# Edge products ahead of pair 0's main product in the opening of four convolution phases

## What is computed

```python
def _layer(x, style, w, b, mw, mb, typ):
    s = style @ mw.T + mb
    weight = SCALE * w * s[:, None, :, None]
    demod = lax.rsqrt(jnp.sum(weight * weight, axis=(2, 3)) + EPS)
    weight = weight * demod[:, :, None, None]
    ...   # 'same' conv; 'upsample': transposed conv and blur; 'downsample': blur and strided conv
x = x + L0_ffn(L0_cond(x, cond_512, ...))   # fp8 quantised product, 1024 x 1024
x = x + L1_ffn(L1_cond(x, cond_512, ...))   # base product and 16 experts of rank 64, top 2
x = x + L2_ffn(L2_cond(x, cond_512, ...))   # base product, 8 experts of rank 16, sparsemax gate
x = x + L3_ffn(L3_cond(x, cond_512, ...))   # low-rank gated (silu) ffn, 1024-256-5504-256-1024
```

## Time and profile before

| | us |
|---|---|
| three executions: median (lowest to highest) | 2113.85 (2109.53 to 2119.47) |
| the profiled execution, its own time | 2111.62 |
| its span, from first to last instruction | 2109.6 |
| TensorE busy | 1958.6 (93% of the span) |
| VectorE, ScalarE, GpSimd busy | 1302.2, 960.7, 374.2 |
| mean granted TensorE clock | 0.971 of full speed |

### The profile page before, as it was taken

The page is one execution under the profiler, slowest core; times in us unless marked ns, Lnnn a source line. Parts: engine busy times, 40 slices in busy tenths (PEclk is TensorE's granted clock), DMA queues, the critical chain, the costliest instruction groups (busy, mean ns, idle before and its releaser), DMA issues. The chain is left out here.

```text
span 2109.6 us, 31997 instructions
## 1 busy us (share of the span) xinstructions
PE 1958.6 (93%) x10128; PEld 1661.1 (79%) x10128; DVE 1302.2 (62%) x2326; ACT 960.7 (46%) x1547; POOL 374.2 (18%) x457
## 2 busy tenths in 40 slices
PE   4899968799999979998899999988999999999999
PEld 4677733699999877887688888877888778878886
DVE  6888888867776753336766666656555433343343
ACT  4477754455545431113444444424666544433442
POOL 4122211211111100002111111112121222222221
PEclk9899989899999989998899999998999999999999
DMA  7566646322112254434211121223333211142114
GB/s 195 179 183 184 177 155 227 108 74 76 60 60 78 62 174 141 144 118 147 94 60 60 60 70 61 64 63 118 100 100 108 89 47 45 52 141 85 50 45 163
DMA packets 118608, 222.30 MB, mean 105 GB/s; under 512 B 18336, under 2 KB 65184, under 8 KB 117792
## 3 DMA queue, kind: packets, MB, share of 16 engines
q1 hardware_dynamic: 102048, 212.36, 32.1%
q10 hardware_dynamic: 16512, 9.31, 1.6%
HBM read 159.04 MB, written 62.59 MB: 105 GB/s over the span
## 5 line engine op out<-in xcount | busy, mean ns | idle before, releaser
L125 POOL TENSOR_TENSOR rows<-l_EY,ones 128x4 f32<-128x4 f32 x128 | 36.0, 281 | 780.9 <-ACT rows L1331 420.4
L2647 DVE SCALAR_TENSOR_TENSOR f_prod<-ps,b,f_gate 128x512 f32<-128x512 f32 (+1 forms) x88 | 66.0, 750 | 171.6 <-ACT f_gate L2587 171.6
L2688 POOL TENSOR_TENSOR x_lo<-f_prod,x_hi 128x512 fp32r<-128x512 f32 (+1 forms) x88 | 104.9, 1192 | 290.5 <-ACT x_hi L2594 290.5
L2517 PE MATMUL ps<-pt_hi,v_hi 128*128 128x512 f32 (+1 forms) x352 | 138.7, 394 | 2.3 <-PEq L631 1.7
L2517 PE MATMUL ps<-pt_lo,v_hi 128*128 128x512 f32 (+1 forms) x352 | 138.3, 393 | 0.0
L2517 PE MATMUL ps<-pt_hi,v_lo 128*128 128x512 f32 (+1 forms) x352 | 137.7, 391 | 0.0
L1079 PE MATMUL ps<-l_u_hi,l_g_hi 128*128 128x512 f32 x272 | 115.2, 424 | 20.2 <-DVE l_u_lo L1535 10.2
L2587 ACT ACTIVATE f_gate<-ps,b 128x512 f32<-128x512 f32 (+1 forms) x88 | 60.5, 688 | 158.8 <-PE ps L2517 158.8
L1559 DVE SCALAR_TENSOR_TENSOR rows<-ps,dem3e,l_middle 128x512 f32<-128x512 f32 x60 | 45.1, 751 | 119.5 <-ACT l_middle L1300 97.2
L125 POOL TENSOR_TENSOR XE<-rows,ones 128x8 f32 (+1 forms) x96 | 21.0, 242 | 531.3 <-DVE rows L1769 256.1
L1079 PE MATMUL ps<-l_u_lo,l_g_hi 128*128 128x512 f32 x272 | 111.1, 408 | 0.0
(11 more groups left out here) (402 smaller groups left out, 5819.7 us busy)
## 6 DMA issues: line engine op xcount, KB each, us to landing
x<-rows SPq DMA_DIRECT2D x64, 512.0 KB, 2.9
xin<-x SPq DMA_DIRECT2D x96, 256.0 KB, 4.1
rows<-x SPq DMA_DIRECT2D x48, 512.0 KB, 4.0
out<-rows SPq DMA_DIRECT2D x32, 512.0 KB, 2.6
v<-in_ffn_v SPq DMA_DIRECT2D x84, 128.0 KB, 2.6
xin<-in_x SPq DMA_DIRECT2D x16, 512.0 KB, 5.4
xb<-in_x SPq DMA_DIRECT2D x16, 512.0 KB, 3.3
x<-xb SPq DMA_DIRECT2D x16, 512.0 KB, 2.6
```

The lines of the kernel that those rows point to most:

```text
L125: return g.tensor_tensor(dst, src, one.broadcast_to(src.shape), ALU.mult)
L2517: mm = nc.tensor.matmul(ps[0:m, 2 * g + gu, :], v1sp[ws][:, s, r, gu, 0:m], pt[ms][:, r, cols], start=(k == 0), stop=(k == 5))
L2647: v.scalar_tensor_tensor(prod[0:m, g, :], ps[0:m, 2 * g + 1, :], b1[0:m, 1, bass.ds(2 * i + g, 1)], gate[0:m, g, :], ALU.add, ALU.mult).th ...
L2688: nc.gpsimd.tensor_tensor(asp[1][0:m, g, :], prod[0:m, g, :], asp[0][0:m, g, :].bitcast(F32), ALU.subtract).then_inc(al_ready, 1)
```

## The change

- TensorE's `edges_p` writes to banks 7 and 4 in place of 5 and 6 (VectorE reads it there), and waits for both halves of pair 0's `l_u_lo` (`ul_ready`) in place of `g_summed`.
- TensorE's order in the opening becomes `conv0_half(1, 0)`, `edges_p`, `conv0_half(1, 1)`, `edges_v`, `main_half(0, 0)`, `weights_a(2)`, `edges_y`, `main_half(0, 1)`, `weights_g(1)`.
- VectorE does `edges_p` ahead of `split_g(0)`, and `edges_y` ahead of `read_u(1, ...)`.
- GpSimd's first piece of weights waits for `gl_ready` of pair 0.
- ScalarE splits the first weight piece after `cross_g(0)` and not before it; in layers 1 to 3 the pieces that were split between `cross_g(1)` and `split_h(0)` come after it, on ScalarE and VectorE.

```diff
@@ TensorE, edges_p
                 pe.wait_ge(ue_ready, n)
-                pe.wait_ge(g_summed, g0 + 1)
+                pe.wait_ge(ul_ready, 2 * g0 + 2)
...
-                                ps[:, 5 + h, 0:NP * 3 * PW].rearrange("p (n k) -> p n k", k=PW),
+                                ps[:, 7 - 3 * h, 0:NP * 3 * PW].rearrange("p (n k) -> p n k", k=PW),
@@ TensorE, iteration, first
                     conv0_half(1, 0)
                     edges_p()
-                    main(0)
+                    conv0_half(1, 1)
                     edges_v()
-                    conv0_half(1, 1)
+                    main_half(0, 0)
                     weights_a(2)
                     edges_y()
+                    main_half(0, 1)
                     weights_g(1)
@@ ScalarE
             split_x(1)
-            some_chunks(1)
             cross_g(0)
-            some_chunks(1)
+            some_chunks(2)
             split_g(0)
@@ ScalarE, first_pair
                 cross_g(1)
-                if layer > 0:
-                    some_chunks(2 if fast else 1)
-                else:
+                if layer == 0:
                     split_g(1)
                 split_h(0)
-                if layer > 0:
-                    some_chunks(1)
-                    if not fast:
-                        split_g(1)
+                if layer > 0 and not fast:
+                    split_g(1)
                 some_chunks(len(chunks))
@@ VectorE, edges_p
-                        src = ps[rows, 5 + h, 0:NP * 3 * PW].rearrange("p (n s k) -> p n s k", s=3, k=PW)
+                        src = ps[rows, 7 - 3 * h, 0:NP * 3 * PW].rearrange("p (n s k) -> p n s k", s=3, k=PW)
@@ VectorE
             split_x_half(1, 1)
-            split_g(0)
             some_maxima(1)
@@ VectorE, first_pair
                 edges_p()
+                split_g(0)
                 read_a(1)
...
                 edges_v()
+                edges_y()
                 if not fast:
                     read_u(1, 0)
                     read_u(1, 1)
-                edges_y()
...
-                some_chunks(2 if fast else 1)
                 split_h(0)
@@ GpSimd
+            if len(chunks) > 0:
+                pool.wait_ge(gl_ready, g0 + 1)
             for k in range(min(POOL_CHUNKS, len(chunks))):
                 chunk(k)
```

## The result

The changed kernel takes 2123.88 us (median of 19 runs, 2119.80 to 2131.89); the kernel before, run beside it 19 times, 2115.39. The medians differ by 8.5 us; the ratio of the runs is 1.0044, 95% interval 1.0032 to 1.0055, which is 9.3 us. The forecast was 2123.6, +9.7 us over the median of 2113.85 known then. The profiled execution took 2123.05 us with a span of 2121.0, against 2111.62 and 2109.6 before: +11.4.

What follows compares the result with a forecast made beforehand. VectorE, never idle in the opening, was taken to bound the kernel. Layer terms 4.0 + 0 + 3.0 + 2.7 gave +9.7 us over the 2113.85 median, 2123.6 us; forecast's own range 2119 to 2128, whole range 2112 to 2132.

Steps and rivals of the forecast that it cites:

- Up to `ve_ready`: VectorE's chain from layer start to `ve_ready`: shifts of 0, -0.5, +2.4 and +0.15 us in layers 0 to 3.
- The signs named: Profile signs: no wait ahead of `edges_p`, stretched `split_z` and first piece, two TensorE waits of 2 to 6 us per opening.
- The turns of the two engines: GpSimd and VectorE alternate instruction by instruction outside PSUM; each GpSimd weight piece takes 2.37 us.
- Rival 2: GpSimd's pieces cost VectorE nothing, `ve_ready` comes earlier; -6.3 us, 2107.6 us; chance 0.12.
- The second half on the path: Half product between `edges_y` and `weights_g(1)`: +2.84 us at full clock; 0.78 us of low-clock loss moves, adding nothing there.
- rival 1: Second halves and `weights_g(1)` run cold, losing up to 2.8 us each; +17.7 us in all, 2131.6 us; chance 0.18.
- Layer by layer: Delay of pair 1's start per opening: +4.0, 0, +3.0 and +2.7 us in layers 0 to 3.
- the pieces that leave `split_h(0)`: Layer 1: two weight pieces leave VectorE's way to `split_h(0)`, -2.35 us.
- The stall: Layer 2: pair 1's `l_g_lo`, 3.59 us beside GpSimd's residual sum in place of 1.40, escapes it; -2.2 us.
- The loops: Pair loops: TensorE has no DMA wait, so what pair 1 loses at its start is carried to the end in full.
- rival 3: Loops of layers 0 and 2 absorb the delay; half the sum, +4.8 us, 2118.7 us; chance 0.15.

Runs made afterwards that it cites:

- a1: The changed kernel without GpSimd's wait for `gl_ready`, so its weight pieces start as early as in the kernel before; 1.0005 of the kernel before.
- a3: The changed kernel with no weight piece on GpSimd; VectorE splits all, two ahead of `edges_v`, four behind `edges_y`; 0.9995 of the kernel before.
- a7: The changed kernel with 20 added matmuls ahead of `edges_y` in layers 1 and 2, in the wait for `l_h_lo`; 1.0039 of the kernel before.
- a6: The changed kernel with the later weight pieces back ahead of `split_h(0)` on ScalarE and VectorE in the fast layers; 1.0049 of the kernel before.
- b1: The kernel before with one part of the change, GpSimd's pieces waiting for `gl_ready`; 1.0008 of the kernel before.
- b2: The kernel before with no weight piece on GpSimd, VectorE splitting all of them; 0.9980 of the kernel before.
- c1: All pieces on VectorE; layers 0 and 3 with the kernel before's order, banks and first wait, layers 1 and 2 with the change's; 0.9959 of the kernel before.
- c2: As c1, but layers 1 and 2 have the whole product ahead of `edges_y` and 20 added matmuls ahead of `edges_v`; 0.9964 of the kernel before.
- a8: As a4, with 20 added matmuls into bank 3 ahead of `edges_v` in every layer; 0.9945 of the kernel before.
- a4: The changed kernel with no piece on GpSimd and pair 0's whole product between `edges_v` and `edges_y`; 0.9980 of the kernel before.

## Why the prediction was right, and where it was not

**Up to `ve_ready`: right.** Forecast 0, -0.5, +2.4 and +0.15 us; measured -0.37, -1.20, +1.82 and -0.23. All four are 0.4 to 0.7 us early. In layers 1 and 3, 0.5 and 0.4 of that lie between the ends of `l_g_lo` and `l_h_lo`, where I had added the pieces' time and VectorE's own in full. The signs named came: next to no wait ahead of `edges_p`, `split_z` and the first piece stretched, waits of 4.8 to 5.7 us at line 989 and 1.4 to 5.6 at line 1003 (the forecast said 2 to 6; layers 0 and 3 lie under that). The turns of the two engines, read off one stretched `x_lo`, are borne out by `a1` and, with 4.06, 4.75 and 1.43 us against 4.0, 4.5 and 1.1, by `a3`. Rival 2 (the pieces cost VectorE nothing) is out.

**The second half on the path: right in kind, too small in size.** The step was "+2.84 us at full clock", with the 0.78 us of `weights_g(1)`'s low clock that "moves and adds nothing". From `ve_ready` to the first transpose it took 3.88, 3.82 and 4.17 us more in layers 1 to 3. The halves behind the longer waits lost 1.5 to 1.8 us each, of which `weights_g(1)` gave back 1.0 and 1.3 in layers 1 and 2, where it had been cold before, and nothing in layer 3, where it had been warm. In these three layers that is the mechanism of rival 1 at a half to two thirds of the 2 us per layer it was given; `a7` shows it by taking it away. So the term was sized 1.0 to 1.3 us too small in each of them.

My argument for the small size was that a wait of 1.33 us had not brought the lower level. It rested on layer 3 alone. The same trace has waits of 1.33 us at `edges_y` in layers 1 and 2 as well, and behind them `weights_g(1)` (line 1059) ran largely cold:

```profile
397.12 0.42 PE L1003 MATMUL ps<-l_h_hi,c_hi 128*128 128x192 f32 x1 [1.33 <-DVE l_h_lo L1622]
...
997.36 0.42 PE L1003 MATMUL ps<-l_h_hi,c_hi 128*128 128x192 f32 x1 [1.33 <-DVE l_h_lo L1622]
```

```profile
399.00:403.00 4.00, 2.73 (x12) 2.70 (x12) 0.66 0.01 2
999.20:1003.00 3.80, 3.02 (x12) 2.89 (x12) 0.57 0.01 2
```

Read with all four layers, the kernel before already had three of four `weights_g(1)` cold in part, and rival 1 deserved more than its 0.18. The Trainium skill's rule that was weighed (page "TensorE: Matmul & The Clock Gate", section "What's actually happening") says that throttled is the default and activity releases it; the forecast took from it that every half behind such a wait starts cold. Two of four did in this profile, in layers 1 and 2, where `edges_y` was cold too (2.88 and 2.87 us). In layer 3 `edges_y` ran warm behind its wait of 1.74 us (2.35 us), and the clock fell only within the half: its first matmul took 0.44 us, the third 0.63:

```profile
1457.82 0.44 PE L1079 MATMUL ps<-l_u_hi,l_g_hi 128*128 128x512 f32 x1
1458.07 0.61 PE L1079 MATMUL ps<-l_u_lo,l_g_hi 128*128 128x512 f32 x1
1458.48 0.63 PE L1079 MATMUL ps<-l_u_hi,l_g_lo 128*128 128x512 f32 x1
```

**Layer by layer.** Layer 0: forecast +4.0, measured +2.91, since its half ran at 2.4 GHz in this profile. Four other kernels have this same opening in layer 0 (`a1`, `a3`, `a6`, `a7`) and show 46.5 to 47.0. But the kernel before's own 42.70 is at the low end too: the four others with its layer 0 (`b1`, `b2`, `c1`, `c2`) show 42.65, 44.27, 43.19 and 43.47. Between the means of five and five it is +3.3. Layer 1: 0 forecast, +0.55 measured, from three parts that each came: `ve_ready` -1.2, the half +3.9, the pieces that leave `split_h(0)` -2.3 (forecast -2.35). Layer 2: +3.0 forecast, +4.08 measured. The stall shrank, by 1.85 of the 2.2 us, to hold against the 3.59 of the earlier trace rows:

```profile
1021.68 1.74 DVE L1584 SCALAR_TENSOR_TENSOR l_g_lo<-l_g_f,s_u,l_g_hi 128x512 fp32r<-128x512 f32 x2 [2.21 <-ACT l_pairs_hi L1325]
```

The half was 1.0 dearer there than its 2.84. Layer 3: +2.7 forecast, +2.94 measured, where +4.17 of the half stood against an `ffn(0)` that took 4.3 us to pair 1's product in place of 5.3, with a granted clock of 0.69 over it in place of 0.51. The sum was met because errors of 1 us each way cancelled: -1.1, +0.6, +1.1 and +0.2 us in layers 0 to 3. That the total came within 1 us is luck; that it lies near 10 is the mechanism.

**The loops.** I had the shift carried to the end in full. In sum it was, and the measured 1.0032 to 1.0055 (+6.8 to +11.6 us) leaves out rival 3's +4.8; layer by layer it wasn't, as the +1.5, -3.2, +1.1 and +1.5 us above show. Single profiles wander by 2 us in layers 1 and 2, and layer 0's opening by 1.6 and 1.4 us over five profiles of the same code. So a distance from one profile is good to about 1.5 us in an opening and 2 us at a layer's end, and the small differences above are no more than that.

## What to carry to other kernels

When a wait is removed, follow the engine that is waited for to its end: here VectorE had almost no pause, so TensorE's wait came back one step later, and a transferred piece of work (half a product) then stood on the path. Put movable work into the longest wait as a whole: the same half, moved ahead of `edges_y`, was worth 10 us, the whole loss. Look at every layer's row before you call a wait harmless. And ask of each helper engine what it costs its neighbour: three weight pieces on GpSimd held VectorE up for longer than VectorE needed to split them itself, and taking them off GpSimd helped the kernel before as well.

## What the runs showed of the hardware

A wait on TensorE has a second price, the clock behind it, and filling it with useless matmuls can pay where TensorE's own work is what the rest waits for: 20 matmuls ahead of `edges_v` took that step from 3.25 to 2.08 us, and with them the kernel went from 0.9980 to 0.9945 of the kernel before. `a8` against `a4` is that edit alone. In `a7` the clock came up as well, but the time gained isn't clear of the noise.

The same opening meets the clock differently from run to run. Layer 0's second half follows a wait of 1.4 us at line 1003 in the changed kernel (2.97 us at 2.4 GHz, above) and 1.53 us in `a7_wait_filled`, whose layer 0 is the same code; there it took

```profile
78.00:84.00 6.00, 4.51 (x12) 3.39 (x12) 0.72 0.19 71
```

1.5 us more. With `a3`, `a1` and `a6`, which have that opening too, the five waits are 1.42, 1.53, 1.93, 2.43 and 2.60 us and the halves behind them take 2.97, 4.51, 4.28, 3.68 and 3.40: the half does not get dearer with the wait. In the last two `edges_y`, which stands between wait and half, took the first share of the lower clock (2.65 and 2.81 us in place of 2.35). So no wait of this length may be called harmless from one profile, and the price may fall due a step later than the wait. The Trainium skill, page "TensorE: Matmul & The Clock Gate", section "What's actually happening", says of its own measurement that the point at which the clock changes varies from run to run; these rows agree with that.
